# Cross attention: scores from split operands, with the keys' and queries' low parts made by GpSimd

## The reference, cut to what matters

```python
x  = fp8_roundtrip(clip(layernorm(hidden) / qx_in_scale))     # 16 x 112 x 512
q  = (x * qx_in_scale) @ wqx.T * wqx_scale                    # 16 heads of 128
k, v = split(ctx @ w_kv_x.T)                                  # 8 groups of 128, from 16 x 375 x 512
q, k = head_layernorm(q) * qxln_w + qxln_b, head_layernorm(k) * kxln_w + kxln_b
p  = softmax(q @ k.T / sqrt(128))                             # per head, 112 x 375
cat = p @ v                                                   # -> fp8 round trip -> projection, added to x
```

## Time and profile before

| what | value |
|---|---|
| time, median of 3 runs | 3532.51 us (3528.98 to 3533.45) |
| the profiled execution's own time | 3518.53 us |
| its span, first to last instruction | 3516.8 us |
| granted TensorE clock, mean over the span | 0.969 |
| PE busy | 3249.5 us, 92% |
| DVE busy | 2386.7 us, 68% |
| ACT busy | 1724.9 us, 49% |
| POOL busy | 793.6 us, 23% |

### The profile page before, as it was taken

The page is one execution under the profiler, slowest core; times in us unless marked ns, Lnnn a source line. Parts: engine busy times, 40 slices in busy tenths (PEclk is TensorE's granted clock), DMA queues, the critical chain, the costliest instruction groups (busy, mean ns, idle before and its releaser), DMA issues. The chain is left out here.

```text
span 3516.8 us, 50927 instructions
## 1 busy us (share of the span) xinstructions
PE 3249.5 (92%) x17776; PEld 2635.9 (75%) x17776; DVE 2386.7 (68%) x6147; ACT 1724.9 (49%) x4169; POOL 793.6 (23%) x936
## 2 busy tenths in 40 slices
PE   5858998997999999999999989999989979998999
PEld 4647877885787888778777867888868757776788
DVE  5997878786666666767667757899765555557433
ACT  5984455444344334443344333788537755452222
POOL 0004444452222222332222224000223310000000
PEclk9879999999999999999999999999999989999999
DMA  6121010002000000210000016999820124543000
GB/s 234 29 61 32 1 49 25 1 27 77 21 21 30 21 23 20 85 38 22 21 21 30 20 42 223 362 404 398 318 60 2 49 107 137 152 138 120 13 12 19
DMA packets 121167, 304.67 MB, mean 87 GB/s; under 512 B 42336, under 2 KB 45920, under 8 KB 115152
## 3 DMA queue, kind: packets, MB, share of 16 engines
q1 hardware_dynamic: 114752, 283.74, 23.0%
q0 software_dynamic: 6160, 17.67, 1.7%
HBM read 255.32 MB, written 45.35 MB: 85 GB/s over the span
## 5 line engine op out<-in xcount | busy, mean ns | idle before, releaser
L42 PE MATMUL bank<-w,cross_ctx_part 128*125 128x512 f32 x1536 | 519.8, 420 | 2.8 <-DVE cross_kn L1179 2.8
L42 PEld LDWEIGHTS bank<-w,cross_ctx_part 128*125 128x125 f32 x1536 | 283.4, 187 | 83.9 <-DVE cross_kn L1179 8.5
L1087 ACT ACTIVATE cross_prob<-bank,cross_neg_max 112x375 f32<-112x375 f32 x256 | 147.0, 574 | 347.5 <-DVE cross_neg_max L1185 347.5
L42 PE MATMUL bank<-w_low,cross_ctx_part 128*125 128x512 f32 x768 | 303.2, 395 | 0.0
L1185 DVE TENSOR_REDUCE cross_neg_max<-bank 112x1 f32<-112x375 f32 x256 | 134.2, 525 | 208.8 <-PE bank L947 205.7
L42 PE MATMUL bank<-moe_wt,moe_zT 128*128 128x448 f32 x1176 | 262.1, 371 | 0.6 <-DVE moe_wt L1872 0.6
L1872 DVE TENSOR_TENSOR moe_wt<-moe_raw,moe_wt 128x1792 fp32r<-128x1792 f32 (+1 forms) x111 | 231.6, 2108 | 14.5 <-ACT moe_wt L1767 13.5
L42 PE MATMUL bank<-mlp_zT,mlp_signs 128*128 128x512 f32 (+1 forms) x1024 | 221.0, 369 | 6.2 <-DVE mlp_zT L2620 6.2
L42 PEld LDWEIGHTS bank<-moe_wt,moe_zT 128*128 128x128 f32 x1176 | 213.5, 188 | 15.5 <-DVE moe_wt L1872 0.8
L42 PE MATMUL bank<-w,self_xq 128*128 128x512 f32 (+1 forms) x464 | 196.8, 424 | 22.6 <-DVE w_low L601 21.3
L1767 ACT ACTIVATE moe_wt<-moe_raw 128x1792 fp32r<-128x1792 f32 (+1 forms) x111 | 196.8, 1775 | 28.5 <-DMA moe_raw<-in_moe_w 16.8
(11 more groups left out here) (436 smaller groups left out, 8131.4 us busy)
## 6 DMA issues: line engine op xcount, KB each, us to landing
moe_raw<-in_moe_w SPq DMA_DIRECT2D x74, 896.0 KB, 7.4
moe_raw<-in_moe_w SPq DMA_DIRECT2D x37, 1024.0 KB, 8.3
stream<-in_L1f SPq DMA_DIRECT2D x32, 768.0 KB, 7.7
cross_ctx_raw<-in_ctxT SPq DMA_DIRECT2D x32, 750.0 KB, 4.3
wide_ctxT<-in_ctxT SPq DMA_DIRECT2D x16, 750.0 KB, 4.2
wide_ctx_rows<-in_ctx SPq DMA_DIRECT2D x16, 750.0 KB
expert_rows<-a_zeros SPq DMA_DIRECT2D x1, 8960.0 KB, 25.7
moe_zrow<-expert_rows SPq DMA_DIRECT2D x35, 256.0 KB, 7.8
```

The costliest lines, as they stand in the source:

```text
L42: mm = pe.matmul(out, a, b, start=first and n == 0, stop=last and n == len(pairs) - 1)
L1087: op = act.activation(prob[:, t % SLOTS, i, :], score_bank(t)[0:S, i * NK:(i + 1) * NK], ACT.Exp, bias=neg_max[:, h:h + 1], accum_out=tota ...
```

## The change

All of it is in `normed_attention`, and nothing changes where `own` is true. In the cross attention:

- PE: `turn` is cut in two. `turn_queries(b)` comes first in the step, ahead of unit 5, and `turn_keys(b)` stays where `turn` was, between units 6 and 7. The banks of the turned pieces change (`TBANK`). A score is a `product` of three matmuls on rounded operands, with 376 columns instead of 375 (one column of zeros is put behind the keys, once). The first score waits for the low part of the first key piece, scores 2 and 6 for later pieces. `project_out` waits until the second key piece is taken from bank 6.
- ACT: every turned piece is written twice, full (`qT`, `kT`) and rounded (`qT_high`, `kT_high`). The queries are taken at the start of the step (`split_queries`), the keys where they were. In a spread step it rounds `spread_qT` in one instruction.
- POOL: it subtracts the rounded from the full numbers (`qT_low`, `kT_low`, over the full ones), after it has copied the rows to be spread. Its order in a step becomes: the two query pieces, `round_cat(g - 1)`, the four key pieces, the roots.
- `clipped` and `magic` lie in the room of `probT`, and the last step's in `qn`.

```diff
-    TBANK = [2, 3, 4] if own else [6, 7, 5, 3, 2, 4]
+    TBANK = [2, 3, 4] if own else [2, 3, 5, 6, 4, 7]
...
+            qT_high, kT_high = sb("qT", [P, H, P], F32R), sb("kT", [P, GR, NK + 1], F32R)
+            qT, qT_low = raw_and_low(k, ctx, "cross_qT", [P, H, P])
+            kT, kT_low = raw_and_low(k, ctx, "cross_kT", [P, GR, NK + 1])
...
+            def turned_by(g, n):
+                pool.wait_ge(s["turned_raw"], turned_no(g, n))
+                pool.wait_ge(s["turned_ready"], turned_no(g, n))
+
+            def queries_low(g, n):
+                turned_by(g, n)
+                heads = slice(4 * n, 4 * n + 4)
+                pool.tensor_copy(spread_qT[:, heads, spread_rows(g)], qT[:, heads, S:]).then_inc(s["spread_ready"], 1)
+                pool.wait_ge(s["spread_ready"], 2 * tiles(g) + n + 1)
+                pool.tensor_tensor(qT_low[:, heads, :], qT[:, heads, :], qT_high[:, heads, :].bitcast(F32), ALU.subtract)\
+                    .then_inc(s["turned_low"], 1)
+
+            def spread_queries_low(g):
+                pool.wait_ge(s["spread_high"], g // GROUP + 1)
+                pool.tensor_tensor(qT_low[:, :, 0:S], spread_qT, qT_high[:, :, 0:S].bitcast(F32), ALU.subtract)\
+                    .then_inc(s["spread_low"], 1)
+
+            def keys_low(g, n):
+                turned_by(g, n)
+                pool.tensor_tensor(kT_low[:, n - 2, 0:NK], kT[:, n - 2, 0:NK], kT_high[:, n - 2, 0:NK].bitcast(F32), ALU.subtract)\
+                    .then_inc(s["turned_low"], 1)
...
             def step(g, one_more):
...
+                if not own:
+                    if spread(g):
+                        spread_queries_low(g)
+                    for n in range(0 if spread(g) else 2):
+                        queries_low(g, n)
+                    if g:
+                        round_cat(g - 1)
+                    for n in range(2, TG):
+                        keys_low(g, n)
...
-                if g != STEPS - 1:
+                if own and g != STEPS - 1:
                     round_cat(g)
...
-            def turn(b):
-
-                if not own:
-                    wait(pe, s["cat_scaled"], 2 * b)
+            def turn_queries(b):
                 for g in range(0 if spread(b) else 2):
-                    pe.wait_ge(s["normed"], norm_no(b, g))
+                    pe.wait_ge(s["normed"], norm_no(b, LU - 1 if not own and b == 0 else g))
                     for h in range(4):
                         mm = pe.transpose(ps[TBANK[g]][:, h * P:(h + 1) * P], qn[:, 4 * g + h, :], k.ident[:])
                     mm.then_inc(s["turned_in_psum"], 1)
+
+            def turn_keys(b):
+
+                if not own:
+                    wait(pe, s["cat_scaled"], 2 * b)
                 pe.wait_ge(s["normed"], norm_no(b, LU - 1))
...
+                if not own and not at_end:
+                    pe.wait_ge(s["turned_raw"], turned_no(b + 1, 3))
+                    pe.wait_ge(s["turned_ready"], turned_no(b + 1, 3))
...
             def scores(b, t):
+                if not own:
+                    if b == 0 and t == 0:
+                        pe.wait_ge(s["padded"], 2)
+                    if t == 0 and spread(b):
+                        pe.wait_ge(s["spread_low"], b // GROUP + 1)
+                    if t in (0, 2, 6):
+                        pe.wait_ge(s["turned_low"], turned_no(b, (2, 4, 4, 5)[t // 2]))
+                    if t >= 3:
+                        pe.wait_ge(s["exp_done"], NS * b + t - 2)
+                    mm = product(pe, score_bank(t)[0:S, 0:NK + 1], [q[:, t, 0:S] for q in (qT_high, qT_low)],
+                                 [key[:, t // 2, :] for key in (kT_high, kT_low)], True, True)
+                    mm.then_inc(s["scores_in_psum"], 1)
+                    return
...
+                    turn_queries(b)
                     unit(b, LU)
                     if not first:
                         weigh_values(b - 1, GR - 1)
                     unit(b, LU + 1)
-                    turn(b)
+                    turn_keys(b)
                     unit(b, LU + 2)
...
+            def split_turned(b, n):
+                act.wait_ge(s["turned_in_psum"], turned_no(b, n))
+                for first, to in ((qT, kT), (qT_high, kT_high)):
+                    out = to if n >= 2 else first
+                    out, at = (out[:, 4 * n:4 * n + 4, :].rearrange("p h t -> p (h t)"), ln_q) if n < 2 else (out[:, n - 2, 0:NK], ln_k)
+                    op = act.activation(out, ps[TBANK[n]][:, 0:out.shape[1]], ACT.Identity, scale=head_ln[:, at:at + 1],
+                                        bias=head_ln[:, at + 1:at + 2])
+                    op.then_inc(s["turned_raw" if first is qT else "turned_ready"], 1)
+
+            def split_queries(b):
+                wait(act, s["spread_ready"], 2 * tiles(b))
+                if spread(b):
+                    act.activation(qT_high[:, :, 0:S], spread_qT, ACT.Copy).then_inc(s["spread_high"], 1)
+                else:
+                    split_turned(b, 0)
+                    split_turned(b, 1)
...
+                if not own:
+                    split_queries(b)
                 if one_more:
                     cast(b + 1)
...
                     take_values(b, 0)
                     take_values(b, 1)
-                take_turned(b)
+                    for n in range(2, TG):
+                        split_turned(b, n)
                 take_values(b, KT - 1)
```

More of the change, by code:

```diff
@@ L842, in step @@
                 half = half_of(g)
-                if not spread(g):
+                if own and not spread(g):
                     keep_spread(g)
+                if not own:
[7 more added lines that the diff above has]
+                        keys_low(g, n)
                 for n in range(LU if one_more else 0):
@@ L855, in step @@
                     k.clear_past_semaphores(pool)
+            for part in () if own else (kT_high, kT_low):
+                pool.memset(part[:, :, NK:].bitcast(F32), 0.0).then_inc(s["padded"], 1)
             for n in range(LU):
@@ L943, in scores @@
                 queries = spread_qT if spread(b) else qT
-                keys = spread_kT if own and spread(b) else kT
+                keys = spread_kT if spread(b) else kT
                 for i in range(HS):
@@ L1070, in take_turned @@
                     wait(act, s["spread_ready"], tiles(b))
-                for n in range(2 * spread(b), 0 if own and spread(b) else TG):
+                for n in range(0 if spread(b) else TG):
                     act.wait_ge(s["turned_in_psum"], turned_no(b, n))
```

32 lines of the change are left out of this document (17 added, 15 removed).

## The result

The changed kernel takes 3548.68 us (median of 6 runs, 3544.72 to 3551.05), the kernel before 3532.98 (6 runs, 3528.98 to 3535.39): a ratio of 1.0043, 95% interval 1.0032 to 1.0054. It is slower by 0.43%, where the forecast was no change at 3533 and a range that ended at 3548. The profiled execution of the changed kernel took 3549.16 us, with a span of 3547.4.

A forecast was written before the change was run, and what follows sets the result against it. PE was taken to bound the kernel, except from unit 0's end to unit 4's start, where a DVE, POOL, DVE chain ends together with it. Terms -0.6 + 1.6 - 0.8 + 0.5 = +0.7 us gave 3533, range 3520 to 3548.

The forecast's parts named there:

- Part 1: Scores as three rounded products: 0.116 us less each, nothing won in scores 3 to 7, 0.348 us a step in scores 0 to 2.
- Rivals 2 and 5: 2: loop not bound by DVE and POOL, 3518, 8%; 5: three products take as long as one, 3543, 4%.
- rival 1: Head of a step: the new wait isn't last, so the heads give their 0.348 us; faster, 3523, 12%.
- Part 3: Queries split at the step's start by ACT and POOL: cost nothing, POOL free 0.45 us before DVE's clip.
- Rival 4: POOL's second query subtraction still runs when DVE's clip starts, so the clip waits; slower, 3549, 5%.
- Part 2: Score 0 newly waits for POOL's first key subtraction, taken as 0.85 us: PE stalls 0.33 us in each of 31 steps.
- Head of a step: Stall at score 0 less the gain of scores 0 to 2: -0.02 us, times 31 -0.6 us (-2.1 to +2.9).
- rival 3: Key subtraction ahead of score 0 costs the whole 1.31 us of 512 columns, stall 0.79 us; slower, 3548, 11%.
- Part 4, the steps ahead of a spread step: Step 6 and its three likes, where PE waits for ACT: -0.2 us each, -0.8 in all (0 to -1.9).
- Part 4, step 15: POOL's key subtractions slowed beside DVE's low parts, score 0 some 3 us late: +0.5 us, ends 0 and +3.
- Part 4, the first step: turn_queries(0) waits for the last normalisation at the stage's first step: +1.6 us, ends 0 and +4.

The follow-up runs named there:

- the run with less work in the loop: Changed kernel with the product of the queries' low part and the keys' high part left out in scores 3 to 7: 3536.01 us, ratio 1.0043.
- The fill's variant: Changed kernel plus ten matmuls that nothing reads, on PE ahead of turn 1 in the four steps before a pre-spread step: 3542.61 us, ratio 1.0032.
- step 15's queries: Changed kernel with ACT's split of step 15's spread queries put ahead of its rounding of weights: 3539.85 us, ratio 1.0034.
- the run with key group 0 first: Changed kernel with POOL's subtraction of key group 0 moved between the two operations that round the context: 3526.29 us, ratio 1.0016.

## Why the prediction was wrong

The sum was +0.7 us and the cross attention took 20.2 us more. Two steps failed: the head of a regular step was mis-sized (5.8 us in all), and the irregular steps of Part 4 were priced without what the granted clock does behind a pause (eight falls more, up to 13.7 us). By its steps:

- **Part 1, the price of a product, and where it counts: right.** 0.17 us per matmul. The loop from turn 0 to unit 4 lasts 13.49 us before and after, and the run with less work in the loop shows that it would not have moved for more. Rivals 2 and 5 fell, and rival 1, since the new wait is last.
- **Part 3, the queries at no cost: right.** POOL ended the second query piece at 1053.52, DVE's clip came at 1053.77 and lasted 0.63 us as before. The distance was 0.25 us, not 0.45. Rival 4 fell. Undone alone, it costs 194 us in the two stretches.
- **Part 2, "I take 0.85 ... PE stalls 0.33 us", and "Head of a step: ... -0.02 us": the step that failed first, in its sizes.** The wait, its releaser and the start of the subtraction (3.46 us behind the turned keys, 3.45 predicted) were right. The subtraction takes 1.00 us (median 1002 ns), above the range of 0.80 to 0.96: 2.67 ns per column, where the forecast's 0.85 us took 2.27, near the 2.12 of the 896-column one, and even the 512-column one's rate was too low. The hand-over is 0.04 and not 0.10, so the stall is 0.43. The other term was not in the sum: a first matmul behind a pause costs 0.09 us more. Score 2 brought 0.09 for 0.116, and 0.05 more lie between unit 4 and the next turning. Altogether 0.43 - 0.14 - 0.09 + 0.05 = +0.25 us in step 5 instead of -0.02; over 24 intervals it was 5.8. The text put the point from which rival 3 decides at 1.05 us of subtraction, and its mark in the cycle at 39.1; the cycle came to 38.97, between forecast and rival.
- **Part 4, the steps ahead of a spread step, "-0.2 each": wrong in sign and in kind.** Each grew by 1.6 us. The prediction followed the probabilities' wait to its end and stopped; it had no term for the granted clock, which fell in each of these steps and didn't before. With the wait filled they are 0.1 us above the kernel before. The fill's variant gives back 7.1 us, but 0.9 of them lie where nothing is filled, and steps 6 and 14 kept their clock without a fill in two other variants; only in steps 22 and 30 does the fill gain what they didn't, 1.1 to 1.3 us each.
- **Part 4, step 15, "+0.5, ends 0 and +3": wrong.** Steps 14 to 16 grew by 5.5 us, of which 1.6 are step 14's clock, and a longer fall in step 16 has a share. The prediction looked at POOL's queue and forgot ACT's, where the new rounding of the spread queries lies behind that of the weights; putting it ahead is worth 2.2 to 2.7 us.
- **Part 4, the first step, "+1.6": too small.** It was 3.6, inside its ends. The wait was predicted well, 4.21 for 4.2, and so was its price: turn 1 is 1.42 us late. Another 1.4 us are a fall of the clock behind turn 1's wait, again a term that the sum didn't have.

The uncertain terms all fell on the same side, up to two thirds of the loss by one omission, and a range built around one cause at a time did not reach to where they add up. Rival 3 named the right place and, at 3548, nearly the right time, with a price of 1.31 us that wasn't real: that its time came so near is luck, since less than a third of the loss was the regular head's.

## What to carry over

Before pricing a saving on the busiest engine, find the stretch in which it lies and which chain ends that stretch: three products left out of the head gave 0.41 us a regular step here, and five out of the loop nothing. Where a change adds a wait in front of the busiest engine, put what it waits for first in its queue; one subtraction moved past half of an unrelated rounding was worth the whole wait. And cost each longer pause of PE twice, once as a pause and once as what it may do to the clock behind it, with every irregular step walked through on every engine's queue. When a variant is read, compare first the places that it doesn't touch: two variants won 1.5 us in step 6 and three won 0.9 us in the last step, and none of them had changed anything there.

## What the runs showed of the hardware

- The clock behind a pause isn't given by the pause. In step 6 a wait of 1.62 us in the changed kernel was followed by clocks of 0.70 and 0.80, one of 1.59 us in its second trace by 0.69, and one of 1.59 us in two variants by 1.00. One of these variants (step 15's queries) does nothing different up to that point. In the run with key group 0 first, even 2.48 us in step 22 brought no fall. What decides, the moment or something else, was not tried. Such a fall costs 0.9 to 1.6 us here, so a variant's gain can be off by that much for each place where PE waits.
- GpSimd's subtractions aren't proportional to their columns: 0.59 us for 240, 1.00 for 375, 1.29 for 512 (median 1285 ns), 1.90 for 896. From 375 to 512 a column costs 2.1 ns, from 240 to 375 3.0 (the 240-column one read and wrote other tiles).
- Back to back, rounded matmuls of 376 columns follow each other at 0.17 us; the first behind a pause leads the next by 0.26 at the full clock, and by 0.24 behind turned probabilities without a pause.
